# Cross attention's keys and values made in the self attention's bank of the accumulator, in a four layer model

## The chip, the cores and the metric

The kernel runs on one core of one Trainium2 chip. The metric is device time in microseconds, the median of several runs; less is better.

## The reference, cut to what matters

Eight elements of a batch (`B = 8`), each 256 tokens of width 256 (`S`, `D`), and for each a context of 64 tokens of width 128 (`M`, `C`) pass four layers in float32: a fusion with memory, a decoder layer with two experts, a gated cross attention with a feed-forward part, and the same decoder layer again with other weights. The change touches the decoder layer (layers 1 and 3). Written out:

```python
h = rms_norm(x) * in_w
q, k, v = split(where(vision_token, h @ v_qkv, h @ l_qkv))
ctx = causal_softmax_attention(rotary(q), rotary(k), v)       # 16 heads of 16
x = x + where(vision_token, ctx @ v_dense, ctx @ l_dense)     # "dense"
h = rms_norm(x) * cross_w
ck, cv = split(context @ ckv_w)                               # "memory": [64, 128] each
x = x + softmax_attention(h @ cq_w, ck, cv) @ cdense_w        # 16 heads of 8
h = rms_norm(x) * post_w
x = x + where(vision_token, mlp_v(h), mlp_l(h))               # inner width 688
```

Keys and values of the context (`ck`, `cv`) depend on the context alone, so they can be made at any time.

## The kernel before, in words

All activations stay on the chip, in `x_all`. Elements of the first decoder layer are numbered 0 to 7, those of the second 8 to 15. The work is cut into stages, and each stage of each element is a word such as `memory.9` or `first_scores.10.1` (element 10, part 1). The dictionary `ORDER` holds one list of such words for each engine, written out: each engine takes its own list from front to back, and semaphores between stages do the rest. A stage has one function for each engine that takes part. The elements are pipelined: while element e is in self attention, e - 1 is in cross attention, e - 2 in its feed-forward part, and e + 1 or e + 2 makes its q, k, v.

The accumulator has eight banks of 512 columns: four `row_banks` (scores), `att_bank`, `crs_bank` and two `ff_bank`s.

- `att_bank` is used by the norm ahead of q, k, v (`n0_sum`, `n0_spread`, L980 to L995), by `turn_max` (L1066, which transposes the negative maxima that `shift_q` of DVE (L1832) reads) and by `values` (L1095, L1107), in which the context of self attention gathers. ACT copies the latter out, `values_out` (L1583, L1587), whose second part signals `co1`. DVE divides (`context`, L1839), and POOL splits it by expert (`split`, L817, L821, L824), which signals `cv` and `cl`.
- `crs_bank` carries the whole chain of cross attention, in order: `memory` (L1114: one matmul for the keys, L1122, and two for the values, L1124; each float32 matmul is two instructions, so six in all), its copies by ACT (`cross_k_out`, L1589, L1593, signals `ck`) and DVE (`cross_v_out`, L1847, four copies at L1858, the last signals `cv3`), `dense` (L1127, matmuls in `to_experts`, L951, at L963 and L956), added to x by `attended` (L1861), the norm (`crs_add` L775, `crs_sum` L1132 at L972, `crs_mean` L1867, `crs_rstd` L857, `crs_spread` at L977, `cross_y`, which scales at L1779), `cross_q` (L1140), `cross_first` (L1146), `cross_max` (L1873), `cross_turn_max` (L1161, L1165), `cross_shift` (L1884, L1887), `cross_second` (L1168, L1176), `cross_exp` (ACT, L1610), `cross_values` (L1180, L1186), `cross_context` (L1890: reciprocal L1892, product L1894), `cross_project` (L1191, L1194), `crossed` (L1896), a second norm with the same stages and the number 1, and `post_y` (L1900, which signals `py` when it has read the bank for the last time).
- The feed-forward part (`up` L1197, at L1218, L1223 and, for its last tile, L1228; `down` L1246, L1253; `late_up`, `late_down` for the last quarter of the tokens) uses the `ff_bank`s, as do q, k and v (`v` L1021, L1025).

`memory` of element e waits until `py` of element e - 1 is there, as the bank is then free; `dense` of e waits for `cv3` of e and for `cl`. `n0_sum` (L980), `turn_max` (L1066) and `a_center` (L1338) wait for `co1` of an earlier element before they write `att_bank`.

The middle layer (stages `a_` and `b_`) uses gelu on ACT (L1712) and exp (L1684). The matmuls of an expert that an element does not need are skipped in blocks by a register test, the same before and after.

## Time and profile before

| | us |
|---|---|
| median of 3 runs | 1356.5 |
| the three runs | 1348.32, 1357.5, 1356.5 |
| the profiled execution, its own time | 1357.66 |
| its span in the trace | 1355.7 |
| mean granted clock of TensorE in it, of full speed | 0.979 |

Engines are PE (TensorE matmul), PEld (its weight load, which overlaps), DVE (VectorE), ACT (ScalarE), POOL (GpSimd). A busy share is an average over the whole span. A wait is the idle time of an engine just before an instruction, put down to what released it. PEclk is the clock that was granted to TensorE, as a share of 2.4 GHz. L12 is line 12 of the kernel before. In a timeline the number in brackets is the idle time before the row; "x16" means that 16 like instructions are merged.

### The profile page before, as it was taken

The numbers are of one execution on the slowest core, as the hardware profiler recorded it, in microseconds if no ns is written. First come the engines' busy times: TensorE is split into PE (matmuls) and PEld (weight loads), VectorE is DVE, ScalarE is ACT, GpSimd is POOL, SyncE is SP. The second block draws the span as 40 slices with busy tenths as digits, with TensorE's granted clock in tenths as the row PEclk, the third lists the DMA queues.
The fourth block names the chain that finished last, engine by engine and source line by source line (L and its number), as shares of the span: only waits on it lengthen the run. The fifth ranks groups of instructions, "written<-read, shape, count | busy, mean of one in ns | idle before, by whom it ended". The sixth has DMA issues, their size and how long they took to land.

```text
span 1355.7 us, 25963 instructions
## 1 busy us (share of the span) xinstructions
PE 1303.4 (96%) x10931; PEld 1052.5 (78%) x10931; DVE 756.0 (56%) x1361; ACT 489.5 (36%) x815; POOL 450.9 (33%) x559
## 2 busy tenths in 40 slices
PE   7988899999999999999999999999899999999988
PEld 6875577887887778888888888776678778787767
DVE  4445576566666656454344554346566656666553
ACT  3333323423334233254345543433341432423321
POOL 1233443534434352221121211324434345334332
PEclk9888899999999999999999999999999999999999
DMA  9010000000001001110000000011000000000000
GB/s 324 14 63 1 1 1 2 1 2 1 2 2 48 1 6 56 56 49 1 0 1 1 1 0 1 0 44 41 2 2 1 17 2 1 2 17 2 1 16 17
DMA packets 19901, 27.29 MB, mean 20 GB/s; under 512 B 3432, under 2 KB 15552, under 8 KB 19520
## 3 DMA queue, kind: packets, MB, share of 16 engines
q1 hardware_dynamic: 19008, 24.20, 5.4%
q8 instruction: 99, 1.62, 0.5%
q10 hardware_dynamic: 768, 1.26, 0.3%
q14 instruction: 26, 0.21, 0.1%
HBM read 23.35 MB, written 2.10 MB: 19 GB/s over the span
## 4 chain that ended last, share of the span: by engine, by line
PE 89%; DVE 3%; ACT 3%; POOL 2%; issue 2%; DMA 0%; SPq 0%; ACTq 0%; DVEq 0%; POOLq 0%
PE bank L963 6%; PE bank L1253 5%; PE bank L1218 5%; PE bank L1107 5%; PE bank L1223 5%; PE bank L1470 4%; PE bank L1463 4%; PE bank L1427 4%; PE row_banks L1367 4%; PE row_banks L1090 4%; PE row_banks L1057 4%; PE bank L1025 3%; PE bank L956 3%; PE bank L1242 3%; PE row_banks L1062 2%; PE row_banks L1320 2%
## 5 line engine op out<-in xcount | busy, mean ns | idle before, releaser
L1829 DVE TENSOR_REDUCE room<-row_banks 128x4 f32<-128x512 f32 (+1 forms) x128 | 116.5, 953 | 20.3 <-PE row_banks L1062 19.6
L1581 ACT ACTIVATE room<-row_banks 128x1536 f32<-128x1536 f32 x64 | 92.9, 1451 | 90.2 <-PE row_banks L1090 90.0
L813 POOL TENSOR_SCALAR_AFFINE_SELECT room<-room 128x1024 f32<-128x1024 f32 x64 | 70.4, 1101 | 139.6 <-ACT room L1581 139.6
L1253 PE MATMUL bank<-room,down_w 128*128 128x256 f32 x384 | 94.1, 385 | 0.5 <-DVE room L1929 0.5
L1619 ACT ACTIVATE room<-bank 128x256 f32<-128x256 f32 x96 | 36.2, 383 | 129.6 <-PE bank L1223 126.8
L1843 DVE RECIPROCAL room<-room 128x256 f32<-128x256 f32 x32 | 55.9, 1748 | 45.4 <-ACT room L1587 45.4
L1253 PEld LDWEIGHTS bank<-room,down_w 128*128 128x128 f32 x384 | 69.3, 190 | 13.3 <-issue 3.9
L834 POOL TENSOR_TENSOR room<-room,is_vis 128x192 f32<-128x192 f32 x80 | 44.8, 560 | 102.6 <-DVE room L1915 102.2
L1912 DVE SCALAR_TENSOR_TENSOR room<-room,bank 128x256 f32<-128x256 f32 x96 | 40.0, 416 | 63.7 <-ACT room L1619 63.6
L1090 PE MATMUL row_banks<-room 32*128 32x256 f32 (+1 forms) x1024 | 62.8, 360 | 9.0 <-ACT room L1581 5.3
L1090 PEld LDWEIGHTS row_banks<-room 32*128 32x128 f32 x1024 | 49.2, 192 | 26.5 <-issue 16.1
L887 POOL TENSOR_TENSOR room<-room 128x512 f32<-128x512 f32 x32 | 33.5, 1057 | 98.8 <-DVE room L2031 98.8
L963 PE MATMUL bank<-room,qkv 128*128 128x256 f32 x256 | 64.7, 398 | 1.4 <-issue 1.4
L775 POOL TENSOR_TENSOR room<-room 128x256 f32<-128x256 f32 x32 | 23.6, 739 | 123.9 <-ACT room L1599 123.9
L1057 PE MATMUL row_banks<-room 32*128 32x128 f32 (+1 forms) x1024 | 62.9, 362 | 1.8 <-ACT room L1559 1.3
L1470 PE MATMUL bank<-room,down_w 128*128 128x256 f32 x256 | 62.5, 381 | 0.0
L1599 ACT ACTIVATE room<-x_all 128x512 f32<-128x512 f32 x32 | 20.2, 630 | 115.9 <-DVE x_all L1898 69.2
L1367 PE MATMUL row_banks<-room,wq 128*128 128x256 f32 x256 | 61.3, 384 | 0.1
L1463 PE MATMUL bank<-room,up_w 128*128 128x256 f32 x256 | 59.4, 381 | 0.0
L1427 PE MATMUL bank<-room,wo 128*128 128x256 f32 x256 | 58.3, 380 | 0.0
L1779 DVE SCALAR_TENSOR_TENSOR room<-x_all,vec_t,bank 128x256 f32<-128x256 f32 x96 | 41.7, 476 | 27.0 <-PE bank L977 26.8
L1107 PE MATMUL bank<-room 128*32 128x256 f32 (+1 forms) x1024 | 55.9, 337 | 0.6
(244 smaller groups left out, 3051.1 us busy)
## 6 DMA issues: line engine op xcount, KB each, us to landing
out_x<-wq SPq DMA_DIRECT2D x8, 256.0 KB, 2.5
qkv<-in_L_xattn_v_qkv SPq DMA_DIRECT2D x2, 768.0 KB, 5.6
qkv<-in_L_xattn_l_qkv SPq DMA_DIRECT2D x2, 768.0 KB, 8.6
gate_w<-in_L_xattn_v_gate SPq DMA_DIRECT2D x2, 640.0 KB, 7.5
gate_w<-in_L_xattn_l_gate SPq DMA_DIRECT2D x2, 640.0 KB, 7.2
up_w<-in_L_xattn_v_up SPq DMA_DIRECT2D x2, 640.0 KB, 5.8
up_w<-in_L_xattn_l_up SPq DMA_DIRECT2D x2, 640.0 KB, 6.1
down_w<-in_L_xattn_v_down SPq DMA_DIRECT2D x2, 640.0 KB, 6.1
```

What stands on the lines that cost most here:

```text
L813: pool.affine_select(out=diagonal, in_=diagonal, compare_op=ALU.is_ge, fill=0.0, base=0, pattern=[[0, 8], [1, P]], channel_multiplier=-1)\
L963: pe.matmul(out[:, t * S:(t + 1) * S], w[:, 1, k, at + t * P:at + (t + 1) * P], y_l[:, k, :], start=(t == k == 0), stop=False, skip_group_ ...
L1057: pe.matmul(row_banks[:, j, P * i:P + S * i], q_one[e % 2][par][r, t, i * P:(i + 1) * P], k_one[e % 2][par][r, t, 0:P * (i + 1)], start=(i ...
L1090: last = pe.matmul(row_banks[:, j, S * i:S + P * i], k_one[e % 2][par][r, t, i * P:(i + 1) * P], q_one[e % 2][par][r, t, i * P:S], start=( ...
L1107: last = pe.matmul(att_bank[32 * j:32 * j + 32, at + i * P:at + S], half if of_sums else v_pad[e % 2][:, i, 8 * t + 2 * j + par, :], probs ...
L1253: return pe.matmul(ff_bank[0][:, t * S:(t + 1) * S], down_w[:, f, t * P:(t + 1) * P], hid[:, i, :], start=(i == t == 0), stop=(i == UPS - ...
L1367: last = pe.matmul(row_banks[:, u, j * S:(j + 1) * S], wq[:, k, at:at + P], a_y[:, k, :], start=(k == 0), stop=(k == KT - 1))
L1427: last = pe.matmul(crs_bank[:, t * S:(t + 1) * S], wo[:, k, t * P:(t + 1) * P], a_context[:, k, :], start=(k == t == 0), stop=(k == GT - 1 ...
L1463: last = pe.matmul(ff_bank[(u + 1) % 2][:, j * S:(j + 1) * S], w1[:, k, at:at + P], b_y[:, k, :], start=(k == 0), stop=(k == KT - 1))
L1470: last = pe.matmul(crs_bank[:, t * S:(t + 1) * S], w2[:, k, t * P:(t + 1) * P], b_hid[:, k, :], start=(k == t == 0), stop=(k == GT - 1), s ...
L1581: act.activation(probs[w % 2], row_banks[:, :, 0:3 * P], ACT.Exp).then_inc(*ATT_ACT.does(e, f"exp{w}"))
L1829: last = dve.tensor_reduce(dst, row_banks[:, :, P * i:P + S * i], X, ALU.max, negate=True)
```

## The change

`memory` writes `att_bank` instead of `crs_bank`. It waits for `co1` of its own element, that is until ACT has copied the second half of the context of self attention. `cross_k_out` and `cross_v_out` read the new bank. `dense` no longer waits for `cv3` of its element; it takes over the waits for `py` of the element before and, for element 8, for the last addition of the middle layer. `n0_sum` and `a_center` wait for `cv3` where they waited for `co1`. `turn_max` drops its wait for `co1`; for the last two elements of a layer it waits for `cv3` of the element before (for the others the same follows from `n0_sum`).

The four lists of `ORDER` for PE, ACT, DVE and POOL are rewritten over their whole length. Each holds the same words as before (1150, 645, 723 and 401). `memory.e` moves from a place ahead of `dense.e` to one behind `values.e.3`. Of the lists, the diff below shows the places of PE's at elements 0 and 1, 8 and 9, and 15; after it stand the changes of the stages in full.

```diff
...
-        n0_spread.3 cross_first.0 turn_max.1 second_scores.1.0 cross_turn_max.0 second_scores.1.1 values.1.0
-        second_scores.1.2 values.1.1 second_scores.1.3 cross_second.0 values.1.2 cross_values.0 values.1.3
-        first_scores.2.0 cross_project.0 q.3 crs_sum.0.1 k.3 crs_spread.0.1 first_scores.2.1 memory.1 v.3 dense.1
...
+        turn_max.1 second_scores.1.0 second_scores.1.1 cross_turn_max.0 values.1.0 second_scores.1.2 values.1.1
+        second_scores.1.3 values.1.2 cross_second.0 values.1.3 cross_values.0 memory.1 first_scores.2.0
+        cross_project.0 q.3 crs_sum.0.1 k.3 crs_spread.0.1 first_scores.2.1 v.3 dense.1 first_scores.2.2 up.0.0
...
-        second_scores.8.1 memory.8 values.8.0 second_scores.8.2 values.8.1 second_scores.8.3 q.10 values.8.2
-        first_scores.9.0 values.8.3 v.10 first_scores.9.1 k.10 dense.8 n0_sum.11 first_scores.9.2 crs_sum.8.0
...
+        first_scores.9.0 v.10 memory.8 first_scores.9.1 k.10 dense.8 n0_sum.11 first_scores.9.2 crs_sum.8.0
...
-        cross_second.8 values.9.3 cross_values.8 v.11 cross_project.8 first_scores.10.0 crs_sum.8.1 crs_spread.8.1
-        memory.9 first_scores.10.1 dense.9 first_scores.10.2 up.8.0 n0_sum.12 crs_sum.9.0 first_scores.10.3
+        cross_second.8 values.9.3 cross_values.8 memory.9 cross_project.8 first_scores.10.0 crs_sum.8.1 v.11
+        crs_spread.8.1 first_scores.10.1 dense.9 first_scores.10.2 up.8.0 n0_sum.12 crs_sum.9.0 first_scores.10.3
...
-        late_down.13.0 late_down.13.1 late_down.13.2 crs_spread.14.1 turn_out.13 memory.15 turn_out.12 dense.15
-        up.14.0 crs_sum.15.0 up.14.1 crs_spread.15.0 up.14.2 cross_q.15 cross_first.15 up.14.3 cross_turn_max.15
-        up.14.4 cross_second.15 up.14.5 cross_values.15 down.14.0 cross_project.15 down.14.1 crs_sum.15.1 down.14.2
...
+        down.13.4 down.13.5 crs_sum.14.1 late_down.13.0 late_down.13.1 late_down.13.2 crs_spread.14.1 turn_out.13
+        turn_out.12 dense.15 memory.15 up.14.0 crs_sum.15.0 up.14.1 crs_spread.15.0 up.14.2 cross_q.15 cross_first.15
+        up.14.3 cross_turn_max.15 cross_second.15 up.14.4 cross_values.15 up.14.5 cross_project.15 down.14.0 down.14.1
+        crs_sum.15.1 down.14.2 crs_spread.15.1 down.14.3 down.14.4 down.14.5 up.15.0 up.15.1 up.15.2 up.15.3 up.15.4
...
@@ -987,7 +988,7 @@
                     elif e == B:
                         pe.wait_ge(*A_DVE.did(B - 1, "scaled"))
                     elif e % B > 2:
-                        pe.wait_ge(*ATT_ACT.did(e - 3, "co1"))
+                        pe.wait_ge(*CRS_DVE.did(e - 3, "cv3"))
                     sum_squares(n0_sq, att_bank).then_inc(*N0_PE.does(e, "sumsq"))
 
                 def n0_spread(e):
@@ -1067,8 +1068,8 @@
                     pe.wait_ge(*ATT_DVE.did(e, "max3"))
                     if e % B + 2 < B:
                         pe.wait_ge(*N0_DVE.did(e + 2, "y"))
-                    if e > 0:
-                        pe.wait_ge(*ATT_ACT.did(e - 1, "co1"))
+                    else:
+                        pe.wait_ge(*CRS_DVE.did(e - 1, "cv3"))
                     for t in range(KT):
                         for i in range(TT):
                             at = t * S + i * P
@@ -1112,20 +1113,18 @@
                     last.then_inc(*ATT_PE.does(e, f"pv{w}"))
 
                 def memory(e):
-                    if e == 0:
-                        pe.wait_ge(*X_ACT.did(B - 1, "x"))
-                    else:
+                    pe.wait_ge(*ATT_ACT.did(e, "co1"))
+                    mem = ctx_t[:, e % B * M:(e % B + 1) * M]
+                    pe.matmul(att_bank[:, 0:M], ckv_w[:, 0:C], mem, start=True, stop=True)
+                    for i in range(2):
+                        last = pe.matmul(att_bank[i * M:(i + 1) * M, P:P + C], mem, ckv_w[:, C:2 * C], start=True, stop=True)
+                    last.then_inc(*CRS_PE.does(e, "kv"))
+
+                def dense_out(e):
+                    if e > 0:
                         pe.wait_ge(*CRS_DVE.did(e - 1, "py"))
                     if e == B:
                         pe.wait_ge(*B_DVE.did(B - 1, "x3"))
-                    mem = ctx_t[:, e % B * M:(e % B + 1) * M]
-                    pe.matmul(crs_bank[:, 0:M], ckv_w[:, 0:C], mem, start=True, stop=True)
-                    for i in range(2):
-                        last = pe.matmul(crs_bank[i * M:(i + 1) * M, P:P + C], mem, ckv_w[:, C:2 * C], start=True, stop=True)
-                    last.then_inc(*CRS_PE.does(e, "kv"))
-
-                def dense_out(e):
-                    pe.wait_ge(*CRS_DVE.did(e, "cv3"))
                     pe.wait_ge(*ATT_POOL.did(e, "cl"))
                     to_experts(e, crs_bank, dense, 0, ctx_l, ctx_v, ATT_POOL.did(e, "cv")).then_inc(*CRS_PE.does(e, "dense"))
 
@@ -1339,7 +1338,7 @@
                     pe.wait_ge(*FF_DVE.did(e, "x4"))
                     pe.wait_ge(*FF_DVE.did(e | 1, "xv"))
                     if e == 0:
-                        pe.wait_ge(*ATT_ACT.did(B - 1, "co1"))
+                        pe.wait_ge(*CRS_DVE.did(B - 1, "cv3"))
                     else:
                         pe.wait_ge(*(A_DVE.did(e - 1, "k11") if e % 2 else A_DVE.did(e - 1, "scaled")))
                     center(e, att_bank).then_inc(*A_PE.does(e, "mu"))
@@ -1590,7 +1589,7 @@
                     act.wait_ge(*CRS_PE.did(e, "kv"))
                     if e > 0:
                         act.wait_ge(*CRS_POOL.did(e - 1, "kd"))
-                    act.copy(ck_sb, crs_bank[:, 0:M]).then_inc(*CRS_ACT.does(e, "ck"))
+                    act.copy(ck_sb, att_bank[:, 0:M]).then_inc(*CRS_ACT.does(e, "ck"))
 
                 def crs_square(e, n):
                     act.wait_ge(*CRS_DVE.did(e, ("x2", "x3")[n]))
@@ -1850,7 +1849,7 @@
                         dve.wait_ge(mot_zeroed, 1)
                     else:
                         dve.wait_ge(*CRS_PE.did(e - 1, "cpv"))
-                    src = crs_bank[:, P:P + C].rearrange("p (g n) -> p g n", g=4)
+                    src = att_bank[:, P:P + C].rearrange("p (g n) -> p g n", g=4)
                     dst = cv_pad.rearrange("p (g q) n -> p g q n", g=4)
                     for h in range(2):
                         for i in range(2):
```

## Rows read from the trace of the kernel before

**Rows 1.** The page: busy time of each engine, share of the span, instructions.
```profile
PE 1303.4 (96%) x10931; PEld 1052.5 (78%) x10931; DVE 756.0 (56%) x1361; ACT 489.5 (36%) x815; POOL 450.9 (33%) x559
```

**Rows 2.** Stage windows: length, then busy us (count) PE PEld DVE ACT POOL, PEclk, DMA.
```profile
650.00:700.00 50.00, 50.00 (x269) 44.16 (x268) 19.95 (x36) 22.68 (x36) 7.30 (x8) 1.00 0.00 1
950.00:1000.00 50.00, 45.75 (x480) 34.46 (x478) 30.32 (x51) 17.34 (x27) 20.04 (x24) 0.93 0.01 1
975.00:980.00 5.00, 2.81 (x24) 1.93 (x24) 4.77 (x10) 0.74 (x2) 3.81 (x4) 0.72 0.00 0
980.00:985.00 5.00, 5.00 (x27) 3.77 (x19) 2.12 (x4) 0.00 (x0) 3.78 (x5) 0.60 0.00 0
```

**Rows 3.** PE's waits: who for whom, us in total, times, longest.
```profile
PE row_banks L1090 <- ACT room L1581: 5.3, 13, 1.7
PE bank L972 <- POOL room L775: 4.4, 6, 1.4
...
PE bank L963 <- DVE room L1858: 1.7, 4, 0.9
...
PE bank L1122 <- DVE room L1779: 1.3, 1, 1.3
```

**Rows 4.** Single lines: who waited for L1858; what L1593 waited for.
```profile
  PEld bank L963: 3.3, 5
...
  PE bank L1124: 69.0, 12
```

**Rows 5.** Groups by line, ACT: busy us, mean ns, idle before and releaser.
```profile
L1587 ACT COPY room<-bank 128x512 f32<-128x512 f32 x32 | 18.7, 583 | 18.1 <-PE bank L1107 17.7
...
L1712 ACT ACT_TABLE_LOAD x14 | 18.0, 1283 | 0.2
...
L1684 ACT ACT_TABLE_LOAD x13 | 16.7, 1283 | 0.2
```

**Rows 6.** Timeline of PE, elements 8 and 9: start, length, idle before it.
```profile
966.42 0.64 PE L1186 MATMUL bank<-wo,room 128*32 128x256 f32 x8 [0.55 <-ACT wo L1610]
...
968.29 2.86 PE L1025 MATMUL bank<-qkv,room 128*128 128x256 f32 x12
...
971.94 0.94 PE L1057 MATMUL row_banks<-room 32*128 32x128 f32 x16
...
974.25 0.61 PE L972 MATMUL bank<-mean_w,room 128*128 128x1 f32 x4 [0.84 <-POOL room L775]
975.89 0.43 PE L977 MATMUL bank<-const,room 128*128 128x128 f32 x2 [1.03 <-POOL room L857]
977.62 0.69 PE L1122 MATMUL bank<-ctx_t,ckv_w 128*128 128x64 f32 x2 [1.30 <-DVE room L1779]
```

**Rows 7.** Timeline of all engines, the tail, element 15.
```profile
1291.13 1.27 POOL L824 TENSOR_TENSOR room<-room 128x512 f32<-128x512 f32 x1
...
1292.65 0.43 PE L1122 MATMUL bank<-ctx_t,ckv_w 128*128 128x64 f32 x2
...
1294.96 1.99 PE L963 MATMUL bank<-room,dense 128*128 128x256 f32 x8 [0.92 <-DVE room L1858]
...
1300.04 0.61 PE L972 MATMUL bank<-mean_w,room 128*128 128x1 f32 x4 [0.46 <-POOL room L775]
...
1309.86 0.88 DVE L1887 SCALAR_TENSOR_TENSOR room<-bank,const,room 128x256 f32<-128x256 f32 x2 [0.53 <-PE bank L1165]
...
1316.59 1.13 PE L1253 MATMUL bank<-room,down_w 128*128 128x256 f32 x4
...
1318.89 1.13 PE L1194 MATMUL bank<-room,cd_w 128*128 128x256 f32 x4 [1.17 <-DVE room L1894]
...
1322.27 0.61 PE L972 MATMUL bank<-mean_w,room 128*128 128x1 f32 x4 [1.38 <-POOL room L775]
```

**Rows 8.** Timeline of PE, elements 0 and 1.
```profile
169.00 1.15 PE L1176 MATMUL row_banks<-room 32*128 32x256 f32 x16 [1.65 <-ACT room L1581]
170.08 0.86 PE L1107 MATMUL bank<-room 128*32 128x256 f32 x16
```

More of the change, by code:

```diff
@@ L199 @@
[L199 to L202 removed]
+        x_turn.0 x_turn.1 x_turn.2 x_turn.3 x_turn.4 f_scores.0 x_turn.5 x_turn.6 f_scores.2 f_scores.1 p_trig.0
@@ new lines @@
+        first_scores.3.0 down.0.1 cross_project.1 down.0.2 down.0.3 down.0.4 crs_sum.1.1 first_scores.3.1
+        crs_spread.1.1 down.0.5 q.4 k.4 first_scores.3.2 v.4 dense.2 up.1.0 up.1.1 crs_sum.2.0 first_scores.3.3
+        crs_spread.2.0 up.1.2 n0_sum.5 cross_q.2 up.1.3 n0_spread.5 cross_first.2 up.1.4 turn_max.3 up.1.5
+        second_scores.3.0 cross_turn_max.2 late_up.1.0 second_scores.3.1 values.3.0 second_scores.3.2 late_up.1.2
+        values.3.1 second_scores.3.3 late_up.1.1 cross_second.2 values.3.2 values.3.3 cross_values.2 down.1.0 down.1.1
@@ new lines @@
+        memory.3 down.1.2 down.1.3 cross_project.2 late_down.1.0 late_down.1.1 down.1.4 crs_sum.2.1 down.1.5
+        late_down.1.2 first_scores.4.0 crs_spread.2.1 q.5 k.5 first_scores.4.1 v.5 dense.3 first_scores.4.2 up.2.0
+        crs_sum.3.0 n0_sum.6 first_scores.4.3 crs_spread.3.0 up.2.1 cross_q.3 n0_spread.6 cross_first.3 up.2.2
+        turn_max.4 up.2.3 second_scores.4.0 up.2.4 second_scores.4.1 cross_turn_max.3 values.4.0 second_scores.4.2
+        values.4.1 second_scores.4.3 up.2.5 cross_second.3 values.4.2 values.4.3 cross_values.3 down.2.0 down.2.1
@@ L298 @@
[L298 to L301 removed]
+        second_scores.10.1 cross_turn_max.9 values.10.0 second_scores.10.2 values.10.1 second_scores.10.3 up.8.5
@@ new lines @@
+        cross_second.9 values.10.2 values.10.3 cross_values.9 down.8.0 memory.10 first_scores.11.0 q.12 down.8.1
+        cross_project.9 down.8.2 down.8.3 down.8.4 crs_sum.9.1 first_scores.11.1 crs_spread.9.1 down.8.5 v.12 k.12
+        up.9.0 dense.10 first_scores.11.2 up.9.2 crs_sum.10.0 up.9.1 crs_spread.10.0 n0_sum.13 first_scores.11.3
+        cross_q.10 n0_spread.13 up.9.3 cross_first.10 up.9.4 turn_max.11 up.9.5 second_scores.11.0 late_up.9.0
+        second_scores.11.1 values.11.0 late_up.9.2 second_scores.11.2 values.11.1 cross_turn_max.10 second_scores.11.3
@@ new lines @@
+        late_up.9.1 cross_second.10 values.11.2 values.11.3 cross_values.10 memory.11 down.9.0 down.9.1
+        cross_project.10 down.9.2 down.9.3 late_down.9.0 crs_sum.10.1 late_down.9.1 down.9.4 down.9.5 late_down.9.2
+        crs_spread.10.1 first_scores.12.0 turn_out.8 turn_out.9 dense.11 q.13 first_scores.12.1 k.13 v.13
+        first_scores.12.2 up.10.0 crs_sum.11.0 n0_sum.14 first_scores.12.3 crs_spread.11.0 up.10.1 cross_q.11
+        n0_spread.14 cross_first.11 up.10.2 turn_max.12 up.10.3 second_scores.12.0 up.10.4 second_scores.12.1
@@ new lines @@
+        values.12.0 second_scores.12.2 cross_turn_max.11 values.12.1 second_scores.12.3 up.10.5 cross_second.11
+        values.12.2 values.12.3 cross_values.11 memory.12 first_scores.13.0 down.10.0 cross_project.11 q.14 down.10.1
+        down.10.2 v.14 crs_sum.11.1 first_scores.13.1 crs_spread.11.1 down.10.3 down.10.4 down.10.5 up.11.0 k.14
+        dense.12 n0_sum.15 first_scores.13.2 up.11.1 crs_sum.12.0 up.11.2 n0_spread.15 crs_spread.12.0
+        first_scores.13.3 cross_q.12 up.11.3 cross_first.12 turn_max.13 up.11.4 up.11.5 second_scores.13.0
@@ L454 @@
+        give.15 late_give.15
     """,
     "pool": """
[L456 to L459 removed]
```

575 lines of the change are left out of this document (274 added, 301 removed).

## The prediction

> **What bounds the kernel now.** The first view is the head of the page [rows 1]: PE is busy 1303.4 of 1355.7 us, the next engine (DVE) 756.0. So only what PE has to wait for, or what makes PE slower, can move the time. The stage windows [rows 2] show where that is: in the middle layer 650:700 holds 50.00 us of PE work, but 950:1000, where the last layer starts, holds 45.75, and its granted clock is 0.93 instead of 1.00. The short windows in that stretch show what that 0.93 is: 975:980 has PE busy 2.81 of 5 us at a clock of 0.72, and 980:985 has 5.00 of 5 us at 0.60. After a stretch with waits PE falls from 2.4 to 1.2 GHz for some time although it has work again. That costs 5 x 0.28 + 5 x 0.40 = 3.4 us. The mean granted clock of the run is 0.979 (table above), so all such dips together cost about 0.021 x 1355.7 = 28 us; at 3.4 each that is about eight.
>
> The second view is the list of PE's waits [rows 3]. It is short: the largest entries inside the layers are exp (5.3 us in 13 gaps) and the norms (4.4 in 6), and nearly all others are single gaps. Two entries are what the change is about: a dense projection (L963) that waited for the copies of the cross values (L1858), 1.7 us in 4 gaps, and `memory` (L1122) that waited for the last read of the cross bank (L1779), 1.3 us in 1 gap. The view of line L1858 [rows 4] adds 3.3 us in 5 gaps of the weight load, which lie before the same matmuls: 3.3 + 1.7 = 5.0 us, partly the same gaps twice, is the most this wait can be. The big number near it, 69.0 us of ACT waiting for `memory` before its copy L1593 [rows 4], is idle time of an engine that is a third busy and costs nothing.
>
> **The change part by part.**
>
> *The six matmuls of `memory`.* They are the same and write another bank: 0 us. The ACT copy (L1593) and the four DVE copies (L1858) are the same and read another bank: 0 us. No row shows them reading this bank; the nearest are ACT's copies of the same bank (L1587, 583 ns for 512 columns) [rows 5], so a cost from that is bounded by 0 and by a few hundredths of a microsecond.
>
> *The wait of `dense` on cv3 goes.* `dense` waited for memory, ACT copy, four DVE copies; for element 15 the chain is 1292.65 to 1294.96 = 2.3 us, with 0.92 us of PE idle at its end [rows 7]. What is late next there is `cl`, POOL's split (L824): 1291.13 + 1.27 = 1292.40, well before [rows 7]. So the four gaps go whole: -1.7 us. Bounds: 0, if something else is as late, and -5.0.
>
> *The wait on `py` moves from `memory` to `dense`.* Its one gap, 1.30 us at 977.62 [rows 6], now falls to `dense`.9, which has `first_scores`.10.1 in front of it (16 matmuls of L1057, 0.94 us as at 971.94 [rows 6], and four more of L1062). With those it is covered, or nearly: -1.3 us; bounds 0 and -1.3. The chain through the cross bank is shorter by one stage of six matmuls and two hops, which helps only where that chain is the late one.
>
> *New wait: `memory` on co1.* It comes after the last `values` and before the next element's scores, so behind it in PE's queue stand `first_scores`, `cross_project` and `down`, all of PE. co1 is a copy of 0.58 us on ACT [rows 5]; in the new order `cross_values` of the element before lies between, from 966.42 to 968.29 less a few hundredths, 1.8 us [rows 6]. 0 us, while that cover stands. If ACT has other work first the gap would be up to 0.6 us each: bounds 0 and 15 x 0.6 = +9.
>
> *New wait: n0_sum(e+3) and turn_max on cv3 instead of co1.* The bank is free some 2.3 us later [rows 7]. In the new order the shortest distance from `memory` to the next user of the bank is element 8: `first_scores`, `k`, `dense`, that is over 6 us of PE; all others have over 10. 0 us; bounds 0 and +2.3 once.
>
> *The orders.* All four lists are rewritten, with the same stages in them. I went through the chains of cross attention, element by element, and compared each chain's length with the PE work that the order puts beside it, before and after. Most are covered in both. What changes:
> - Elements 8 to 9. `v`.11 (2.86 us from 968.29 [rows 6]) stood between `cross_values`.8 and `cross_project`.8, beside DVE's reciprocal and product. Now `memory`.9 alone stands there, 0.5 us against a chain of 2.35, which element 15 shows: `cross_values` ends as the `down` at 1316.59 starts, L1194 comes at 1318.89 [rows 7]: +1.85. `v`.11 now hides the 1.03 us before the spread at 975.89 [rows 6]: -1.03. Together +0.8.
> - Elements 0 and 1. `values`.1.2 goes ahead of `cross_second`.0, whose wait was 1.65 us [rows 8]; it is two groups of L1107 like the one at 170.08 (0.86 us each, overlapping), some 1.3 us: -1.3. But `cross_values`.0 to `cross_project`.0 loses some cover (1.8 against 2.35): +0.5. Together -0.8.
> - Element 5: the sum before its second norm has more beside it; its gap goes: -0.5 (one of the six gaps of the entry L972 [rows 3], whose mean is 0.7; I take 0.5).
> - Element 15, the tail [rows 7]. `cross_second` now follows `cross_turn_max` at once, and the DVE shift of 0.88 us lies bare: +1.1. `cross_second` to `cross_values` loses 0.2 of cover: +0.2. `up`.14.5 instead of `down`.14.0 (1.13) before `cross_project` adds 0.8 of cover to a gap of 1.17: -0.8. Two `down` instead of one before the sum, whose gap is 1.38: -0.9. `memory`.15 behind `dense` fills the 0.46 before the first sum: -0.5. Together -0.9 (the 0.92 of `dense` is counted above).
>
> Sum: -1.7 - 1.3 + 0.8 - 0.8 - 0.5 - 0.9 = -4.4 us. Made against the profiled run, 1357.66 us (span 1355.7 and 2.0 around it), that is 1353.3. The profiled run is 1.2 over the median of 1356.5, so 1352.1; I take 1352.
>
> *The middle layer.* No stage of it is changed, only its order. PE is full there [rows 2], so it is 0 us. One thing can be counted: each change between gelu and exp on ACT loads a table, 14 + 13 times in the trace, 1.28 us each [rows 5]; in the new ACT list there are two changes fewer, 2.6 us of ACT, hidden under PE. The Trainium skill ("ScalarE: Activation LUTs", section on what ACT_TABLE_LOAD costs) says the load is about 1283 ns, with a drain of about 1380 ns behind it. The trace agrees with the first number and not with the second, since the next activation starts as the load ends. By the page two loads would be 5.3 us of ACT; here that would change the sum only if ACT were the bound.
>
> **The rivals.**
>
> *A. The order wins more, through the clock.* The waits at 966 to 978 (0.55 + 0.84 + 1.03 + 1.30 [rows 6]) stand ahead of a dip. If the new order breaks up two of the eight such places, two dips go: 2 x 3.4 = 6.8 on top of 4.4, and the tally of cross attention alone may miss as much as 4 in the other queues. 1356.5 - 15 = 1341. For it: the fast run of the three, 1348.32, shows that this kernel loses more or less to the same dips from run to run. Against it: the waits that open the dips at the start, at the turn of the middle layer and after it hang on norms and exp, which the change leaves alone.
>
> The Trainium skill ("TensorE: Matmul & The Clock Gate", part 1) says the ramp penalty is under 1% of a typical kernel span. The trace has 2.1%, so it does not agree. By the page this rival could win no more than 13 us.
>
> *B. `cross_project` takes the place of `memory`.* The 1.85 us between `cross_values`.8 and `cross_project`.8 come in one piece, with 0.84 still behind it, and the pair `cross_turn_max`/`cross_second` adds 1.1 in the tail. If the gains at `dense` are half what I take (-1.5), if a few `memory` wait for co1 (6 x 0.6 = 3.6), and one dip comes on top (+3.4), it is 1356.5 + 2.95 - 1.5 + 3.6 + 3.4 = 1365. It decides from about two new gaps over 1.5 us in a stretch that has none. For it: the order has less cover in exactly that place. Against it: co1 is short and ACT a third busy.
>
> *C. Nothing.* The cross bank's chain was hidden anyway; 1.7 + 1.3 us are all that rows show, and the orders give back the same. 1356.5.
>
> **How the numbers follow.** Forecast (a small gain, 1347 to 1356): 0.50. A: 0.20. B: 0.17. C: 0.13. The range reaches into A and B: 1340 to 1364; that is the +9 and -5 of the bounds with two dips either way. One per cent, 13.6 us, is about what a measurement of this kernel can tell from no change; its three runs span 9.2 us. Faster by over 1% (under 1343) is most of A: 0.16. Slower by over 1% (over 1370) is B with a second dip: 0.06. The rest, 0.78, is within 1%.
>
> **What would show it.** Right: no PE wait of L963 for L1858; L1122 waits for L1587 or not at all; a new gap of 1 to 2 us before L1194 near 970; no gap of 1.0 before the spread there; in the tail `dense`.15 without a gap, L1176 behind one of about 1 us; 12 and 13 or fewer table loads of gelu and exp; PE's sum of waits 3 to 6 us less, the mean clock within 0.005 of 0.979. Wrong: a mean clock over 0.985 (A); entries of `memory` for ACT over 2 us in all, or a mean clock under 0.975 (B).

## The result: 1338.0 us, 1.15% faster, below the forecast's range

| | before | after |
|---|---|---|
| median of 6 runs each, us | 1354.88 | 1338.03 (1337.25 to 1343.97) |
| ratio | | 0.9885, 95% interval 0.986 to 0.991 |
| profiled execution, us (span) | 1357.66 (1355.7) | 1337.81 (1335.9) |
| its mean granted clock | 0.979 | 0.988 |

The forecast was 1352 with a range of 1340 to 1364. Measured again later beside other runs, the full change gave 1338.66 and a ratio of 0.9898 (0.987 to 0.993). The gain is about 15 us, more than three times the 4.4 that my steps made.

The head of after's page answers to [rows 1]:

```profile
PE 1288.9 (96%) x10931; PEld 1045.4 (78%) x10931; DVE 757.6 (57%) x1361; ACT 488.1 (37%) x813; POOL 452.2 (34%) x559
```

PE is busy for 14.5 us less with the same 10931 instructions. That cannot be removed work; nearly all of it is the same work at a higher clock: 1357.66 x 0.021 = 28.5 us went to the clock in the one execution and 1337.81 x 0.012 = 16.1 in the other, 12.4 less. ACT has two instructions fewer, the two table loads. The stage windows of after (columns as in [rows 2]):

```profile
650.00:700.00 50.00, 50.00 (x278) 43.78 (x277) 23.08 (x43) 20.58 (x34) 8.32 (x10) 1.00 0.00 1
...
935.00:940.00 5.00, 5.00 (x42) 4.41 (x40) 2.60 (x4) 1.45 (x1) 0.48 (x1) 1.00 0.01 3
940.00:945.00 5.00, 4.94 (x93) 3.64 (x95) 0.88 (x2) 2.15 (x2) 1.71 (x2) 1.00 0.01 2
950.00:955.00 5.00, 3.88 (x70) 2.12 (x62) 2.15 (x3) 2.74 (x4) 4.55 (x4) 1.00 0.02 3
955.00:960.00 5.00, 4.11 (x27) 2.51 (x27) 4.09 (x9) 0.63 (x1) 2.02 (x4) 0.66 0.00 0
960.00:965.00 5.00, 5.00 (x40) 4.05 (x41) 3.58 (x7) 1.29 (x5) 3.09 (x3) 1.00 0.00 0
950.00:1000.00 50.00, 47.31 (x548) 34.38 (x540) 35.73 (x58) 20.18 (x32) 22.27 (x28) 0.97 0.01 2
```

The last window shows 47.31 of 50 us busy at 0.97, where [rows 2] had 45.75 at 0.93. What stood at 975 to 985 at 0.72 and 0.60 is one window at 0.66, a loss of 5 x 0.34 = 1.7 us instead of 3.4.

At the start the difference is larger. These windows are of before (not shown ahead of the prediction); nothing in them got a term in my sum:

```profile
45.00:50.00 5.00, 4.58 (x33) 3.60 (x32) 4.17 (x12) 2.29 (x6) 3.15 (x6) 1.00 0.02 5
50.00:55.00 5.00, 5.00 (x32) 4.31 (x31) 3.65 (x16) 0.98 (x3) 1.94 (x3) 0.72 0.00 0
55.00:60.00 5.00, 5.00 (x17) 3.90 (x16) 1.88 (x8) 1.47 (x4) 0.00 (x0) 0.50 0.00 0
60.00:65.00 5.00, 5.00 (x25) 3.92 (x24) 1.02 (x3) 0.45 (x2) 0.00 (x0) 0.76 0.00 0
```

and the same stretch of after:

```profile
50.00:55.00 5.00, 4.97 (x36) 3.97 (x35) 3.23 (x15) 1.67 (x5) 1.39 (x2) 1.00 0.00 0
55.00:60.00 5.00, 5.00 (x32) 4.16 (x32) 1.67 (x7) 1.41 (x4) 0.00 (x0) 1.00 0.00 0
60.00:65.00 5.00, 5.00 (x27) 4.20 (x25) 1.38 (x2) 3.12 (x7) 0.72 (x1) 1.00 0.01 3
```

PE is busy in both, but issues 17 instructions against 32 in 55:60: 1.2 GHz against 2.4. The three windows from 50 on cost before 5 x (0.28 + 0.50 + 0.24) = 5.1 us.

The list of PE's waits in after, beside [rows 3]:

```profile
PE row_banks L1091 <- ACT room L1580: 5.5, 12, 1.7
...
PE bank L1193 <- DVE room L1893: 2.2, 4, 1.6
...
PE bank L973 <- POOL room L776: 1.6, 3, 0.7
```

No dense projection waits for L1857 (before's L1858). In the tail, too, the timeline of after shows what I had listed, beside [rows 7]:

```profile
1290.22 0.44 PE L1164 MATMUL bank<-const,room 128*128 128x128 f32 x2 [0.56 <-DVE room L1880]
1291.63 1.15 PE L1175 MATMUL row_banks<-room 32*128 32x256 f32 x16 [0.97 <-DVE room L1886]
...
1299.04 1.13 PE L1193 MATMUL bank<-room,cd_w 128*128 128x256 f32 x4 [0.23 <-DVE room L1893]
...
1302.42 0.61 PE L973 MATMUL bank<-mean_w,room 128*128 128x1 f32 x4 [0.22 <-POOL room L776]
```

The 0.92 before `dense`.15 and the 0.46 before the first sum are gone; 1.17 became 0.23, 1.38 became 0.22, and 0.97 is new. Of the signs that the prediction named, those on single waits came, and PE's idle time is 5.3 us less (52.3 to 47.0, span less busy time), inside its 3 to 6. The clock's sign failed: 0.988 is over the 0.985 that it had set for rival A.

**Two measures for all runs.** Every run lists its time and granted clock. I split it: time x clock is its *time at full clock* (work and waits), time x (1 - clock) its *clock loss*. Means over the timed runs, in us (the clock is listed to 0.001, so a single run's split is uncertain by 0.7). Each kernel was timed beside before on the same chip, and its ratio is taken to those runs; the chip was not the same for all rows:

| kernel | runs | at full clock | clock loss | median | ratio (95%) |
|---|---|---|---|---|---|
| before, beside the others | 67 | 1329.1 | 24.5 | 1353.1 to 1353.6 | |
| neutral | 12 | 1329.3 | 23.7 | 1353.19 | 0.9998 (0.9975, 1.002) |
| bank | 8 | 1326.8 | 19.0 | 1344.85 | 0.9951 (0.9928, 0.9973) |
| prologue | 8 | 1327.8 | 18.5 | 1345.30 | 0.9947 (0.9924, 0.9970) |
| bank_prologue | 6 | 1323.6 | 19.5 | 1343.39 | 0.9916 (0.9892, 0.9939) |
| prologue_late | 5 | 1324.5 | 18.3 | 1341.76 | 0.9901 (0.9883, 0.9919) |
| after_old_prologue | 6 | 1325.2 | 17.0 | 1342.62 | 0.9916 (0.9893, 0.9939) |
| lists_first | 6 | 1322.4 | 18.8 | 1341.85 | 0.9892 (0.9872, 0.9912) |
| after, after_2 | 12 | 1321.8 | 17.3 | 1338.03, 1338.66 | 0.9885, 0.9898 |
| after_fsum | 5 | 1322.2 | 16.6 | 1339.36 | 0.9880 (0.9859, 0.9902) |
| filled_2 | 6 | 1322.4 | 16.7 | 1338.46 | 0.9897 (0.9871, 0.9923) |
| filled_3 | 7 | 1322.6 | 19.2 | 1340.50 | 0.9921 (0.9894, 0.9948) |
| filled | 12 | 1329.1 | 22.4 | 1352.23 | 0.9981 (0.9961, 1.0001) |
| fsum | 12 | 1329.4 | 21.6 | 1352.56 | 0.9980 (0.9964, 0.9995) |

Before to after: -7.3 at full clock and -7.2 of clock loss. Single runs spread over 17.5 to 28.5 us of clock loss for before and 14.7 to 22.8 for after; at full clock the standard deviation within a row is 0.5 to 1.8 us.

### The profile page after: what moved, and what is told of

It is laid out like the page before. It is cut to its first block, busy times and chain, and to the rows that moved or that the text cites. A ratio compares the mean times of both kernels' runs of the same rounds, so it can differ in the third digit from the quotient of the medians.

```text
span 1335.9 us, 25959 instructions
## 1 busy us (share of the span) xinstructions
PE 1288.9 (96%) x10931; PEld 1045.4 (78%) x10931; DVE 757.6 (57%) x1361; ACT 488.1 (37%) x813; POOL 452.2 (34%) x559
## 4 chain that ended last, share of the span: by engine, by line
PE 88%; DVE 4%; ACT 3%; POOL 2%; issue 2%; ACTq 1%; DVEq 0%; POOLq 0%
PE bank L964 6%; PE bank L1252 6%; PE bank L1217 5%; PE bank L1222 5%; PE bank L1108 5%; PE bank L1462 4%; PE bank L1426 4%; PE row_banks L1366 4%; PE bank L1469 4%; PE row_banks L1091 4%; PE row_banks L1058 4%; PE bank L1026 3%; PE bank L1241 3%; PE bank L957 3%; PE row_banks L1063 2%; PE row_banks L1400 2%
## 5 line engine op out<-in xcount | busy, mean ns | idle before, releaser
L1252 PEld LDWEIGHTS bank<-room,down_w 128*128 128x128 f32 x384 | 69.2, 190 | 12.4 <-issue 3.0
L964 PE MATMUL bank<-room,qkv 128*128 128x256 f32 x256 | 61.7, 384 | 0.1
L1108 PE MATMUL bank<-room,const 128*32 128x256 f32 (+1 forms) x1024 | 54.1, 329 | 0.0
```

Of the source, the lines that this page charges most:

```text
L964: pe.matmul(out[:, t * S:(t + 1) * S], w[:, 1, k, at + t * P:at + (t + 1) * P], y_l[:, k, :], start=(t == k == 0), stop=False, skip_group_ ...
L1108: last = pe.matmul(att_bank[32 * j:32 * j + 32, at + i * P:at + S], half if of_sums else v_pad[e % 2][:, i, 8 * t + 2 * j + par, :], probs ...
L1252: return pe.matmul(ff_bank[0][:, t * S:(t + 1) * S], down_w[:, f, t * P:(t + 1) * P], hid[:, i, :], start=(i == t == 0), stop=(i == UPS - ...
```

## The experiments

**1. Which part? bank, prologue, bank_prologue, after_old_prologue.** The change has three parts that can be built apart: the bank's code, the order of the prologue (all stages before `first_scores`.0.0), and the order of the layers.

```diff
bank:                before + the change's code; old lists, but
-  memory.8 values.8.0 ... values.8.3          (PE)
+  values.8.0 ... values.8.3 memory.8
-  cross_k_out.8 q_out.10 values_out.8.1       (ACT)
+  q_out.10 values_out.8.1 cross_k_out.8
prologue:            before + new lists for the prologue only
bank_prologue:       both
after_old_prologue:  after with old lists for the prologue only
```

> The kernel before with the change's code for the bank (memory writes the self attention's bank, waits on co1, dense waits on py, the readers of the bank wait on cv3) and the old four lists; only memory.8 and the copy cross_k_out.8 stand one place later, behind the last values of element 8, since the new code needs that. Theory 1 (the gain is the prologue's order and the clock dips it takes away): the bank alone gives what my gaps gave, 1 to 4 us, so 1351 to 1354, and the granted clock stays near 0.979. Theory 2 (the gain is the bank: the chain through the cross bank is shorter, and the new lists matter little): 1340 or less, clock over 0.985. Theory 3 (only the lists of the layers matter): no change, 1355.

> The kernel before, bank code and all, with the new order of the fusion prologue alone (the first 69 stages of PE, 57 of ACT, 53 of DVE, 22 of POOL; the rest of the lists is the old one). Theory 1 (prologue): first_scores.0.0 starts near 86.6 us instead of 95.5, the dips at 50 to 65 and at 75 to 85 are gone, and all of it stays until the end: 1345 to 1348, 7 to 10 us less. Theory 2 (bank): 1355, because a start that is earlier by 9 us is given back at the first place where the weights or the norms are late. Theory 3 (the lists of the layers): 1355 likewise.

> The two before together: bank code and the new order of the prologue, the old lists in all layers. Theory 1: 1342 to 1346, the sum of the two single ones, which leaves 4 to 8 us for the lists of the layers. Theory 2: 1338 to 1340, as the full change. Theory 3: 1355 or little less.

> The full change with the old order of the prologue. Theory 1: first_scores.0.0 again near 95.5 us and the dips at 50 to 65 back: 1345 to 1348, 7 to 10 us more than the full change's 1338. Theory 2 and theory 3: 1338 to 1340, as the full change.

Measured (table): all three theories fell as exclusive ones, since each part gains. At full clock the bank gives 2.3 on before; the layers' lists give 1.6 (after_old_prologue against bank) and 1.8 (after against bank_prologue); the prologue 3.2 and 3.4 on kernels with the new bank, 1.3 on before. Of the clock loss, the bank alone takes 5.5 us away and the prologue alone 6.0; two parts together take 5.0 (bank_prologue) and 7.5 (after_old_prologue), all three 7.2 (beside the first two kernels before itself lost 23.5, not 24.5, so 1.0 of each may be the batch). The layers' lists were never built without the bank. Two things that I had expected did not come: the bank's clock did not stay near 0.979 (its mean is 0.986), and with the old prologue put back, after_old_prologue has no dip at 50 to 65.

The bank's waits went as the diff says. The list of PE's waits of the bank kernel (its L956 is before's L963, its L1110 is `memory`):

```profile
PE row_banks L1083 <- ACT room L1572: 5.4, 13, 1.7
PE bank L965 <- POOL room L768: 4.4, 6, 1.4
...
PE bank L1110 <- ACT room L1578: 0.7, 1, 0.7
```

The first two entries stand as in [rows 3]. The entries of `dense` for the cross values (1.7) and of `memory` for the last read of the cross bank (1.3) are gone; `memory` waits once for co1, 0.7. That is -2.3, and the means of the table have -2.3.

**2. Is a dip the order's or the execution's? before_2 to before_4, bank_2, prologue_2, after_2, neutral.** All but the last are copies of kernels already told of, for a further trace; neutral is

```diff
-  memory.15 turn_out.12        (PE, before's list, near 1290 us)
+  turn_out.12 memory.15
```

> The kernel before once more, unchanged, for a second trace of it: the runs of the bank kernel and of the full change with the old prologue have no clock dip at 50 to 65 us, although their instructions are the same as the old ones up to there. Theory 1a (the clock dips at a given place come in some executions and not in others, and my profiled execution of before was a bad one): this trace lacks some of the dips at 50 to 65, 75 to 85, 935 to 950 or 975 to 985, the sum of PE's idle time stays within 2 us of the first trace, and the time is 1348 to 1354. Theory 1b (the dips belong to the order): the same dips at the same places, 1356 to 1358.

> The kernel before with one swap of two neighbours in PE's list near 1290 us (turn_out.12 ahead of memory.15) and nothing else. Both traces of before have a clock dip at 50 to 65 us, which costs 5 us; none of the eight traces of changed kernels has it, and two of those issue the same instructions up to there. All variants with the bank or the prologue lose 17 to 20 us to the clock, before 24.3. Theory H1a (that dip belongs to what before does in its first 60 us): it is in the trace again, the clock loss is 23 to 25 us, the time 1352 to 1356. Rival H1b (it goes with any new build, by a shift of a few tenths of a microsecond against the chip's own clock logic): no dip at 50 to 65, the loss is 18 to 20 us, 1347 to 1349 with no change of the work.

> The full change once more, unchanged, on the chip and beside the runs of the other three, for a second trace. Expected 1338 to 1341, at full clock 1321.9, clock loss 17 to 18 us; no dip at 50 to 65, at 75 to 85 or at 930 to 950. If the dips are chance, one of these three is in this trace; if they belong to the lists, none.

> The kernel before, unchanged, for a third trace. Loss to the clock by place in the traces so far (before, before_2, and neutral, which is the same up to 1290 us): start 5.1, 5.1, 0; 70 to 100 5.1, 3.4, 3.4; 100 to 125 5.1 each; 140 to 170 3.4 each; 860 to 890 3.4 each; 925 to 990 6.8, 6.8, 5.2. Theory (the number of steps at a place is drawn in each execution, the waits there only set between which values): the start is 0 or 5.1, 925 to 990 is 5 to 7. Rival (before always has the dip at the start, neutral was the exception): 5.1 at the start.

> The kernel before, unchanged, for a fourth trace; expectations as for before_3. If both traces have no dip at the start, the dip there is chance, and the rest of the difference in the mean loss (24.4 against 17.3 us) has to come from 925 to 990, where the full change has 0 to 1.7 in three traces.

> The bank kernel, unchanged, for a second trace. Its first trace lost 3.4 at 925 to 990 (before 5.2 to 6.8) and 1.7 each at 140 to 170 and at 860 to 890 (before 3.4). Theory (the bank takes the wait of 1.3 us at 977 away, and so a step of the clock at 925 to 990): 3.4 to 5.1 there again, 3.4 at the two other places. Rival (the bank acts on the whole run, by its timing against the chip's clock logic): 1.7 at the two other places again.

> The prologue kernel, unchanged, for a second trace. Its first one lost 0 at the start, 3.4 at 70 to 100, 5.1 at 925 to 990. Theory (the new prologue has no dip at the start in any execution, and one step less at 70 to 100, since the gap of 1.36 us at 79 is gone): 0 and 1.7 to 3.4. Rival (chance): 5.1 at the start is possible here too.

Clock loss by place, each the sum of 5 x (1 - PEclk) over windows of 5 us:

```text
trace               0-70  70-100  100-125  140-170  860-890  925-990
before               5.1     5.1      5.1      3.4      3.4      6.8
before_2             5.1     3.4      5.2      3.4      3.4      6.8
before_3             5.1     3.4      5.1      1.7      3.5      1.7
before_4             0       5.1      5.2      3.4      3.5      6.8
neutral              0       3.4      5.1      3.4      3.4      5.2
bank                 0       3.4      5.1      1.7      1.7      3.4
bank_2               5.2     5.1      5.1      1.7      1.7      3.4
after_old_prologue   0       5.1      5.1      1.7      3.4      0
prologue             0       3.4      5.2      3.4      3.5      5.1
prologue_2           0       3.4      5.1      3.5      3.4      6.8
bank_prologue        0       3.5      5.2      5.1      3.4      5.2
after                0       1.7      5.1      3.4      3.4      1.7
after_2              0       1.7      5.1      3.4      3.4      1.7
```

Every entry is near 0, 1.7, 3.4, 5.1 or 6.8. The start varies between executions of the same instructions: neutral issues what before issues up to 1290 us, and here is its stretch 50 to 65, to be held beside before's above:

```profile
50.00:55.00 5.00, 4.96 (x34) 3.93 (x34) 3.15 (x13) 1.68 (x5) 1.35 (x2) 1.00 0.00 0
55.00:60.00 5.00, 5.00 (x32) 4.13 (x32) 3.12 (x11) 1.11 (x4) 0.00 (x0) 1.00 0.00 0
60.00:65.00 5.00, 5.00 (x27) 4.18 (x25) 0.60 (x1) 2.77 (x7) 0.00 (x0) 1.00 0.01 3
```

So H1a as written fell (neutral's trace has no dip there), and H1b too (its mean loss is before's, 23.7). So the dip is a matter of chance as long as the lists are the old ones. With the old first half of the prologue's lists it came in 4 of 10 traces (those above, prologue_late and fsum), with the new one in 0 of 10. If the lists made no difference, luck would put all four on the old side in about one case of 23, so that the new ones remove it is likely and not shown. At 925 to 990 before varies from 1.7 to 6.8, the bank kernel twice has 3.4, after twice 1.7. For the bank I had expected 3.4 at the two other places on a second trace; it was 1.7 again, which was the rival's number: that holds at 860, where the seven traces without the bank's code all have 3.4 or 3.5 and fsum, a third one with this code and before's prologue, has 1.7 too. But bank_prologue has the code and 3.4, so the code alone doesn't settle it. At 140 before_3 has 1.7 as well, which can be chance.

A dip also doesn't follow from the gaps ahead of it alone. Before's timeline at the turn to the last layer:

```profile
938.84 0.61 PE L972 MATMUL bank<-mean_w,room 128*128 128x1 f32 x4 [0.72 <-POOL room L775]
944.06 1.13 PE L1143 MATMUL bank<-room,cq_w 128*128 128x256 f32 x4 [0.96 <-DVE room L1779]
945.95 1.66 PE L1157 MATMUL row_banks<-room 32*128 32x256 f32 x16 [0.76 <-ACT room L1603]
```

and that of the bank kernel, whose lists are the same there:

```profile
929.95 0.60 PE L965 MATMUL bank<-mean_w,room 128*128 128x1 f32 x4 [0.71 <-POOL room L768]
933.81 1.13 PE L1134 MATMUL bank<-room,cq_w 128*128 128x256 f32 x4 [0.96 <-DVE room L1770]
935.70 1.15 PE L1148 MATMUL row_banks<-room 32*128 32x256 f32 x16 [0.76 <-ACT room L1594]
```

The gaps agree to 0.01 us; before has 0.70 and 0.66 in the windows at 940 and 945, the bank kernel has 1.00 from 925 to 955:

```profile
940.00:945.00 5.00, 4.04 (x27) 2.49 (x26) 3.39 (x8) 1.52 (x2) 0.69 (x1) 0.70 0.00 0
945.00:950.00 5.00, 4.24 (x25) 3.15 (x25) 4.38 (x6) 1.11 (x3) 0.00 (x0) 0.66 0.00 0
```

**3. Where in the prologue and in the layers? prologue_late, lists_first.**

```diff
prologue_late:  bank + new lists for the prologue's second half only
lists_first:    after up to dense.7 on PE, old lists behind it
```

> The bank kernel with the new order of the second half of the prologue alone (the fusion of elements 4 to 7 and the norms and projections of element 0: PE stages 43 to 69, ACT 35 to 57, DVE 30 to 53, POOL 16 to 22). At full clock (time x granted clock) the bank kernel has 1326.8 us and the one with the whole new prologue 1323.6. Theory 1c (it is the place at which q.0 came behind f_sum.4, with its gap of 1.38 us that hung on no engine, and the norms behind it): 1323.5 to 1324.5 at full clock, so nearly all of the 3.2 us. Rival 1d (it is the first half, where p_vec and x_turn wait for DMAs): 1326 to 1327, no gain.

> The full change up to the end of the first layer (PE's list to dense.7, the others likewise), then the bank kernel's old lists for the middle and the last layer. Full clock times so far: whole change 1321.9, bank and new prologue with old lists 1323.6. My own steps put -0.8 and -0.5 in the first layer, +0.8 and -0.9 in the last, 0 in the middle. Theory (my steps hold): 1322.3 at full clock, 1339 to 1341 in time. Rival (the gain of the lists is in the last layer and at the turn from the middle one): 1323.6 at full clock, and the clock itself lower by the dips at 930 to 950, 1342 to 1344.

Of the prologue's 3.2 the second half gives 2.3 (1326.8 to 1324.5). Of the layers' 1.8, the first layer gives 1.2 (1323.6 to 1322.4) and the rest 0.6 (to 1321.8). My own steps had 1.3 and 0.1. With 5 and 6 runs of the two kernels these means are good to about half a microsecond, so the 0.6 and the 0.9 that is left for the prologue's first half are hardly clear of noise.

**4. Fill the gap that is left: filled, filled_2, filled_3.** After has the gap that I forecast between `cross_values`.8 and `cross_project`.8:

```profile
953.49 0.43 PE L1118 MATMUL bank<-ctx_t,ckv_w 128*128 128x64 f32 x2
...
955.89 1.41 PE L1193 MATMUL bank<-room,cd_w 128*128 128x256 f32 x4 [1.61 <-DVE room L1893]
```

```diff
filled, PE's list alone:
-  memory.9 cross_project.8 first_scores.10.0 crs_sum.8.1 v.11 crs_spread.8.1 first_scores.10.1
+  memory.9 first_scores.10.0 cross_project.8 v.11 crs_sum.8.1 first_scores.10.1 crs_spread.8.1
-  cross_second.15 up.14.4 cross_values.15 up.14.5 cross_project.15 down.14.0 down.14.1 crs_sum.15.1
+  up.14.4 cross_second.15 up.14.5 cross_values.15 down.14.0 down.14.1 cross_project.15 down.14.2 down.14.3 crs_sum.15.1
filled_2: after + the first two lines, and on DVE
-  crs_mean.8.1 maximum.10.0
+  maximum.10.0 crs_mean.8.1
filled_3: filled_2 + the last two lines, and on DVE
-  cross_shift.15 hidden.14.4 hidden.14.3 cross_context.15 hidden.14.5
+  cross_shift.15 hidden.14.3 hidden.14.4 hidden.14.5 cross_context.15
```

> The full change with PE's list alone changed at two places: first_scores.10.0 between memory.9 and cross_project.8 (a gap of 1.61 us in the trace of after), v.11 between cross_project.8 and its sum, first_scores.10.1 ahead of the spread; and in the tail up.14.4 back before cross_second.15 (gap 0.97), up.14.5 before cross_values.15, two downs before cross_project.15, two before the sum. Theory (a gap that is filled comes back whole, and the dip behind it goes too): -1.6 and -1.2 of waits and up to -1.7 of clock, 1334 to 1336. Rival (another gap opens behind, since the stages that filled those places were needed there): 1338, no gain.

> The full change with the part of the last trial at elements 8 to 10 alone, and with DVE's list made to fit: maximum.10.0 ahead of crs_mean.8.1. In the trial that changed PE's list alone the gap before cross_project.8 went from 1.61 to 0.19, but first_scores.10.1 then waited 1.98 us for maximum.10.0, which stood behind crs_mean.8.1 on DVE, and the projection behind it 0.96. Theory (four lists have to fit; the price was DVE's order): both new gaps go, 1320.5 to 1321 at full clock, 1336 to 1338. Rival (first_scores.10.1 is simply too early there, its reader takes 2 us whatever the order): 1323 or more at full clock, 1340 or more.

> The same with the tail refilled too: PE's list as in the first trial (up.14.4 and up.14.5 around cross_second.15, two downs before cross_project.15, two before the sum), and on DVE hidden.14.3, hidden.14.4 and hidden.14.5 ahead of cross_context.15 and in this order, as the kernel before has them. In the first trial up.14.5 waited 3.97 us for hidden.14.3 and the first down after it 3.13. Theory: both go, and the gap of 0.97 before cross_second.15 with them: 1 us less than filled_2, 1319.5 to 1320 at full clock. Rival (exp of element 15 and the tanh of 14.3 to 14.5 share ACT, so a gap stays): no better than filled_2.

filled is 1% slower than after, all the way back to before: 7.3 us more at full clock, which neither side had expected. Its tail:

```profile
1299.07 1.74 PE L1220 MATMUL bank<-room,gate_w 128*64 128x256 f32 x8 [3.97 <-DVE room L1907]
...
1307.64 1.99 PE L1245 MATMUL bank<-room,down_w 128*128 128x256 f32 x8 [3.13 <-DVE room L1907]
```

`up`.14.5 waits for a product (`hidden`.14.3) that stands behind others in DVE's list: 7.1 us of idle time from moves on PE alone. With DVE's list made to fit, these two go, but nothing is won. In filled_2:

```profile
955.69 1.13 PE L1186 MATMUL bank<-room,cd_w 128*128 128x256 f32 x4 [0.20 <-DVE room L1886]
...
961.46 0.94 PE L1051 MATMUL row_banks<-room 32*128 32x128 f32 x16 [1.71 <-DVE room L1821]
...
964.85 3.75 PE L957 MATMUL bank<-room,dense 128*128 128x256 f32 x8 [1.07 <-POOL room L818]
```

1.61 became 0.20, and 1.71 and 1.07 opened behind it: the scores now wait for DVE's maximum, which starts late because a reciprocal of 1.74 us stands before it, and `dense` for POOL's split. filled_3's tail likewise has no 0.97 but 1.65 before `up`.15.0. At both places the chain over the other engines seems to be as long as PE's work beside it. The rivals hold: 1322.4 and 1322.6 at full clock, no better than after's 1321.8.

**5. The gap before q.0: fsum, after_fsum.** In the old prologue PE is idle for 1.36 us before the first projection, and no engine is named:

```profile
79.23 3.53 PE L963 MATMUL bank<-room,qkv 128*128 128x256 f32 x8 [1.36 <-issue]
```

The new prologue has no such gap, and one sum less ahead of it.

```diff
fsum:        bank, PE:  - f_sum.4 f_sum.5 q.0 k.0       + f_sum.5 q.0 k.0 f_sum.4
                   DVE: f_mean.4 behind flip_k.0
after_fsum:  after, PE: f_sum.4 put back before f_sum.5
```

> The bank kernel with f_sum.4 moved on PE from before f_sum.5 to behind k.0 (and its reader f_mean.4 on DVE behind flip_k.0); everything else old. Theory (the gap of 1.38 us before q.0 comes from the eight short matmuls of two sums in front of q.0's register loads, whose time only queued work can cover): the gap is gone or under 0.3, 1325.3 to 1325.7 at full clock against the bank kernel's 1326.8. Rival (the gap belongs to something else that the new prologue changes, such as the weights' arrival or the order of ACT): it stays at 1.3 to 1.4, and the time at 1326.8 or more.

> The full change with f_sum.4 put back before f_sum.5 on PE. Theory: the gap of 1.3 to 1.4 us before q.0 is back, 1323.1 at full clock against 1321.8, time 1340. Rival: no gap, 1321.8, 1338 to 1339.

The theory fell on both sides. The timeline of fsum has the gap, larger than before, and a new one behind it:

```profile
74.43 3.42 PE L956 MATMUL bank<-room,qkv 128*128 128x256 f32 x8 [1.87 <-issue]
...
83.78 0.43 PE L970 MATMUL row_banks<-const,room 128*128 128x128 f32 x2 [1.58 <-POOL room L861]
```

after_fsum, with both sums ahead of q.0, has no gap there and 1322.2 at full clock. It is not the number of sums. prologue_late has no gap either, so the cause lies in the second half's lists.

The traces point to one place, though no run tried it alone. The sum of element 5 waits for POOL's add of its squares (L862), and behind that sum in PE's list come the eight register loads of q.0 (L1000), then the projection. In before the add of element 5 is the second of this row, and ends at 75.99, 1.9 us before PE's sums do:

```profile
74.58 1.41 POOL L862 TENSOR_TENSOR wq<-wq 128x256 f32<-128x256 f32 x2 [19.61 <-ACT wq L1664]
76.93 0.95 PE L972 MATMUL row_banks<-mean_w,wq 128*128 128x1 f32 x8
```

In after it ends at 68.55, 3.4 us before PE's sum:

```profile
67.82 0.73 POOL L863 TENSOR_TENSOR wq<-wq 128x256 f32<-128x256 f32 x1 [3.34 <-ACT wq L1663]
71.50 0.50 PE L973 MATMUL row_banks<-mean_w,wq 128*128 128x1 f32 x4
71.87 1.97 PE L964 MATMUL bank<-room,qkv 128*128 128x256 f32 x8
```

From the end of that add to the projection it is 3.2 to 3.3 us in all nine traces with the gap and 3.3 to 4.0 in all eleven without. So the projection seems to need some 3.2 us from the add, and PE has other work for only 1.9 of them in the old lists. There DVE gates element 5 ahead of element 4 and ACT squares both behind `f_tanh`.5, which makes the add late; the new lists have `f_gated`.4 first and `f_square`.4 ahead of `f_tanh`.5. fsum left the add where it was and took one sum of 0.50 us from the work beside it: its gap is 0.51 larger. after_fsum kept the early add. What fills the 3.2 us the profile doesn't say.

## Why the prediction was wrong

**The steps of cross attention held.** *Dense's wait on cv3 goes, -1.7* and *the wait on py moves, -1.3*: the bank kernel shows both entries gone, less 0.7 for one wait on co1 (bound 0 to +9, taken at 0), together -2.3 at full clock against my -3.0. *The orders* made -1.4; the runs say -1.6 and -1.8. By place: +1.85 before `cross_project`.8 was 1.61; the 1.03 before the spread went; 1.1 in the tail was 0.97; -0.8 and -0.9 there were -0.94 and -1.16; +0.5 at element 0 was 0.20, and the 1.65 there, of which I had taken 1.3, went whole. The sum of bank and layers' lists was forecast at -4.4 and measured at -3.9 (1329.1 to 1325.2, after_old_prologue).

**The step that failed is "the orders".** The text says that all four lists are rewritten and then: "I went through the chains of cross attention, element by element". That is a tally of one sort of stage. The prologue, whose lists are rewritten just as much, got no term. It is worth 3.4 us at full clock (1325.2 to 1321.8). The 1.36 us before q.0 lay open in before's timeline, and I didn't put it into any row. The idle time of PE between 10 and 1330 us falls by 2.1 between the traces of after_old_prologue and after (37.3 to 35.2); the other 1.3 I couldn't place.

**The second failure is the clock, taken at 0 in the sum.** It is 7.2 us, half of the gain. Rival A had the kind right: 1341, "the order wins more, through the clock". That its sum of two dips (6.8) is close to the 7.2 is luck in part: at the place that it names, 925 to 990, the four traces of before lose 5.5 on average and both of after 1.7, so 3.8 come from there and the rest from elsewhere. I wrote against A that the dips at the start hang on waits "which the change leaves alone"; but the change rewrites the prologue's lists too, and the dip at 50 to 65 is one that no trace with the new ones has. And "eight dips of 3.4" was wrong in form: a place loses 1.7 to 6.8, differently in each execution. So was the use of the profiled run of before: with 1357.66 and 28.9 us lost up to 1330 it was at the bad end of a kernel whose mean loss is 24.5. The 13 us by which I capped A rest on the figure of the Trainium skill ("TensorE: Matmul & The Clock Gate", part 1) for the warm-up, which I had set beside the loss of the whole run, 2.1%; it caps no later dips. The range's words don't add up either: 1352 with the +9 and two dips of 3.4 is 1368, not 1364.

**B and C.** B (cross_project takes memory's place) saw the gap that came, 1.61, and its condition for a loss was two new gaps over 1.5 us; only one came between elements 8 and 9, with one dip of 1.7 behind it at 955 to 960; the 0.97 in the tail stayed under. C fell with the ratio's interval.

**The table loads** came out as counted, 13 and 12. They were hidden before and after.

```profile
L1711 ACT ACT_TABLE_LOAD x13 | 16.7, 1283 | 0.2
...
L1683 ACT ACT_TABLE_LOAD x12 | 15.4, 1283 | 0.2
```

**Open.** The cause of the 7.2 us of clock is not shown: what decides in a given execution whether a dip follows the same gaps, and why the bank's code goes with a lower loss at 860 us, in three traces, where these show before's waits. I have mean losses and a few traces each. By the means, bank and prologue together (19.5) lose no less than either alone. What the table does show is that waits and clock loss go together: the four kernels at 1329 us at full clock (before, neutral, filled, fsum) lose 21.6 to 24.5, all the others, at 1321.8 to 1327.8, lose 16.6 to 19.5. So the 7.3 us of waits may have brought the 7.2 of clock with them, at no one place.

## What to carry to other kernels

When a diff rewrites an order written by hand, price every stretch that it rewrites, not only the stages that the title names: the windows of 5 us over the whole span, of time busy and of granted clock, show in one look where waits and dips lie. Split each run into time at full clock and clock loss; the first repeats with a standard deviation of 0.5 to 1.8 us and shows differences of 2 us in a few runs, the second is drawn anew each time. And four lists are one thing: a few moves on PE alone cost 7 us, and where a gap is filled, ask first whether the chain behind it is the longer one. Where a wait has no releaser ("issue"), look at what the stages ahead of it in the same list waited for, as with POOL's add here.

## What the runs showed of the hardware

- The clock loss comes in steps near 1.7 us at recurring places, and the number of steps differs between executions of the same program (start of before: 0 or 5.1; 925 to 990: 1.7 to 6.8). I had taken a dip for a property of the gaps before it. The Trainium skill ("TensorE: Matmul & The Clock Gate", part 1) says that the warm-up of one and the same kernel varies from run to run; these traces show such a variation for the dips in the middle of a kernel too. The same part puts the penalty of that ramp under 1% of a typical span. All later dips together cost more here: 1.8% before (24.5 of 1353.6) and 1.3% after (17.3 of 1339.1).
- The recorded clock misses the slow start. It is 1.00 in every window up to 50 us of every trace, but four matmuls of 128x128 take 1.06 us at 6.88 (L911) and 0.63 us at 23.06 (L933), both in before. This part, alike in all kernels, is counted as time at full clock above.
- PE can be at 1.2 GHz in a stretch where it is busy: before at 50 to 65 us, 5.00 of 5 in each window at 0.72, 0.50 and 0.76, with 4.58 of 5 busy in the one before it.
- A change that alters nothing in the first 100 us and 2.3 us of waits in all went with 5.5 us less clock loss (24.5 to 19.0), and one that swaps two neighbours near the end with next to none (23.7).
